# Window attention between two group norms and a 3x3 convolution: v as the weights of the values matmuls, four head pairs side by side

## What is computed

```python
x = x + _L0_conv_ref(_gn(x), qkv_weight, qkv_bias, proj_weight, proj_bias, rel_pos_table)   # attention
x = x + _L1_conv_ref(_gn(x), w, pruning_mask)                                              # 3x3 conv, 128 to 128

# _L0_conv_ref: shifted 7x7 windows; 8 x 8 windows an image, N = 49 tokens each, 8 heads of hd = 16 channels
x = jnp.roll(x, (-3, -3), axis=(1, 2))              # then cut into windows
qkv = x @ qkv_weight.T + qkv_bias                   # q, k, v of each window and head: 49 x 16
q = q * hd ** (-0.5)
attn = jnp.einsum('whnd,whmd->whnm', q, k) + rel_pos_bias + shift_mask
attn = jax.nn.softmax(attn, axis=-1)
x = jnp.einsum('whnm,whmd->whnd', attn, v)          # "values": 49 x 16 for each window and head
x = x @ proj_weight.T + proj_bias                   # windows are put back and rolled back
```

## Time and profile before

| | |
|---|---|
| median of 3 runs | 3634.08 us (3633.68 to 3637.13) |
| profiled execution: its own time | 3628.35 us |
| profiled execution: span, first to last instruction | 3626.5 us |
| granted TensorE clock, mean over the span | 0.995 of full speed |
| busy share PE / DVE / ACT / POOL | 94% / 84% / 73% / 64% |
| instructions in the trace | 141183 |

### The profile page before, as it was taken

One profiled execution on the slowest core, in us unless ns is written; L12 is line 12 of the kernel. 1 busy time (PEld: TensorE's weight loads), 2 busy tenths in 40 slices (PEclk: granted clock), 3 DMA queues, 4 the chain that ended last, 5 costly groups with the idle time before them and its releaser, 6 DMA issues.

```text
span 3626.5 us, 141183 instructions
## 1 busy us (share of the span) xinstructions
PE 3415.0 (94%) x57227; PEld 2799.3 (77%) x57227; DVE 3045.9 (84%) x7552; ACT 2630.5 (73%) x5857; POOL 2322.2 (64%) x3674
## 2 busy tenths in 40 slices
PE   2999999999999999999999999999999999999997
PEld 1778778778778778778777778777778778788785
DVE  5788888888888888888888888888888888888885
ACT  1777777777777777777777777777777777777772
POOL 4476666766666766666766666766667766657763
PEclk9999999999999999999999999999999999999998
DMA  2011101111101111101111111111111111111001
GB/s 57 20 30 33 33 25 30 36 33 36 33 25 30 36 33 36 33 23 33 35 34 35 28 28 33 33 35 36 28 28 33 33 36 33 30 25 33 18 18 29
DMA packets 213331, 113.75 MB, mean 31 GB/s; under 512 B 8784, under 2 KB 212688, under 8 KB 212688
## 3 DMA queue, kind: packets, MB, share of 16 engines
q1 hardware_dynamic: 212688, 104.72, 11.0%
HBM read 53.31 MB, written 51.38 MB: 29 GB/s over the span
## 4 chain that ended last, share of the span: by engine, by line
PE 51%; DVE 23%; POOL 12%; issue 11%; ACT 2%; SPq 0%; DVEq 0%; POOLq 0%; DMA 0%; ACTq 0%
PE conv_ps L994 14%; PE qkv_ps L875 10%; PE attn_ps L913 7%; PE probsT_ps L899 7%; PE scores_ps L888 5%; DVE s_sb L743 4%; POOL s_sb L404 3%; DVE plane_lo L755 3%; PE misc_ps L875 2%; DVE s_max L748 2%; DVE x_b L791 2%; PE misc_ps L961 2%; PE misc_ps L957 2%; PE misc_ps L951 2%; POOL x_n L444 1%
## 5 line engine op out<-in xcount | busy, mean ns | idle before, releaser
L404 POOL TENSOR_TENSOR s_sb<-s_sb,s_max 113x392 f32<-113x392 f32 x1024 | 1027.7, 1004 | 1127.6 <-DVE s_max L748 1123.2
L899 PE MATMUL probsT_ps<-ident,probs 113*128 113x113 f32 x4096 | 586.4, 265 | 72.6 <-ACT probsT L466 72.5
L460 ACT ACTIVATE probs<-s_sb 113x392 f32<-113x392 f32 x1024 | 551.6, 539 | 128.3 <-POOL s_sb L404 124.8
L432 POOL TENSOR_TENSOR plane<-x_n 128x224 f32<-128x224 f32 x896 | 601.3, 692 | 18.7
L913 PEld LDWEIGHTS attn_ps<-v,probsT 128*49 128x49 f32 x16384 | 465.4, 125 | 181.9 <-issue 160.3
L748 DVE TENSOR_REDUCE s_max<-s_sb 113x8 f32<-113x392 f32 x1024 | 574.6, 561 | 35.3
L527 ACT COPY v<-qkv_ps 64x256 f32<-64x256 f32 (+2 forms) x1280 | 393.6, 327 | 287.7 <-PE qkv_ps L875 281.6
L466 ACT COPY probsT<-probsT_ps 128x392 f32<-128x392 f32 x1024 | 489.5, 478 | 144.6 <-PE probsT_ps L899 140.4
L743 DVE TENSOR_TENSOR s_sb<-scores_ps,bias 113x392 f32<-113x392 f32 x1024 | 564.7, 551 | 8.1 <-PE scores_ps L888 8.1
L913 PE MATMUL attn_ps<-v,probsT 128*49 128x34 f32 x16384 | 566.5, 214 | 3.5 <-DVE o_sb L719 0.6
L899 PEld LDWEIGHTS probsT_ps<-ident,probs 113*128 113x128 f32 x4096 | 431.4, 141 | 129.3 <-ACT probs L460 86.0
(11 more groups left out here) (142 smaller groups left out, 6706.9 us busy)
## 6 DMA issues: line engine op xcount, KB each, us to landing
x_in<-in_x_dram SPq DMA_DIRECT2D x224, 224.0 KB, 2.8
out_dram<-x_out SPq DMA_DIRECT2D x224, 224.0 KB, 2.5
x_b<-in_L_conv_w_dram SPq DMA_DIRECT2D x1, 576.0 KB
x_b<-L_conv_pruning_mask_dram SPq DMA_DIRECT2D x1, 576.0 KB
...
```

Of the source, the lines that this page charges most:

```text
L404: nc.gpsimd.tensor_tensor(s, s, top, ALU.subtract).then_inc(sub_ready, 1)
L432: last = nc.gpsimd.tensor_tensor(plane[:, t % 2, j], *sums[j])
L460: nc.scalar.activation(probs[0:QP, slot % 2, :, :, 0:N], s_sb[0:QP, slot % 4], ACT.Exp)\
L899: last = nc.tensor.transpose(probsT_ps[:, w * 128:w * 128 + QP], probs[0:QP, u % 2, w].rearrange("p e m -> p (e m)"), ident[0:QP, 0:QP])
```

## The change

The order of operands in the values product is swapped, and the work is done a row of windows at a time.

- `values(row)` stands once a row of windows, at the end of the row's unit 5 (`VALUES_AT`), for all four head pairs. `v` of one window and pair (32 columns) is the weights, and `probsT` (49 columns) moves. Each pair has its own 32 columns of the array and its own 32 partitions of `attn_ps`, so the output has channels on the partitions at once. 32 matmuls do the outputs. 16 more, with the constant `head_ones` as weights and the `probsT` of two windows (98 columns) moving, add up the softmax's sums for `SUM_PARTS` = 4 pairs of windows in 98 columns of `attn_ps`; `head_ones` puts the sums of part `a` and head `e` on its own partition of the pair's 32 (each four times over).
- DVE takes one reciprocal of 128 x 98 a row (L751). SP writes every fourth partition of it to a DRAM scratch, `recip_dram`, and reads it back into `recip_wide`, spread over the 16 channels of each head and the 392 tokens. DVE multiplies the outputs by it into `o_sb` (L756, unit 8, `NORMED_AT`).
- The `ot` jobs are gone: no transposes. ACT's copy to `oT_hi` stands in the middle of unit 8 and waits for `o_ready`; DVE's `oT_lo` is in unit 9 (`SPLIT_AT`), and `proj` stays at the end of unit 9.
- `probsT` has six slots in place of two, since a row's four units are kept. For the room, `x_out` has two slots in place of seven, and two setup buffers lie inside `plane`. The ones in `v` are gone; POOL writes `head_ones` in the setup.

The core of the diff:

```diff
-LAG_T, LAG_PV = 2, 3
+LAG_T = 2
+VALUES_AT, NORMED_AT, SPLIT_AT = 5, 8, 9
 MID, END = 0, 1
-OT_AT, PROJ_AT = 7, 9
+PROJ_AT = 9
...
+def row_of(i, u, first):
+
+    r, rest = divmod(u - first, PAIRS)
+    turn, r = divmod(r, ROWS)
+    return (i + turn) * ROWS + r if rest == 0 and live(i, turn) else None
...
-        v = sb("v", [128, 2, NWIN, PAIRS, VW])
+        v = sb("v", [128, 2, NWIN, PAIRS, 2 * HD])
         s_sb = sb("s_sb", [128, 4, WP, 2, N])
         s_max = sb("s_max", [128, 4, 2 * WP])
         probs = sb("probs", [128, 2, WP, 2, ODD])
-        probsT = sb("probsT", [128, 2, NWIN, N])
-        recip = sb("recip", [128, 2, 2 * WP, 2])
-        o_sb = sb("o_sb", [128, WP, C])
+        probsT = sb("probsT", [128, PT_SLOTS, NWIN, N])
+        recip = sb("recip", [128, SUM_COLS])
+        recip_wide = sb("recip_wide", [128, RT])
+        o_sb = sb("o_sb", [128, WIN, W])
         oT_hi = sb("oT_hi", [128, WIN, W], F16)
         oT_lo = sb("oT_lo", [128, WIN, W], F16)
+
+        recip_dram = nc.dram_tensor("recip_dram", (2, HEADS, RT), F32).ap()
...
+                    row = row_of(i, u, VALUES_AT + 1)
+                    if row is not None:
+
+                        sp.wait_ge(recip_ready, row + 1)
+                        need(sp, recip_wide_in, 16 * (row - 1))
+                        sp.dma_start(recip_dram[row % 2].rearrange("h (a n) -> (h a) n", a=SUM_PARTS),
+                                     recip[0:128:4, :]).then_inc(recip_out, 16)
+                        need(sp, o_ready, row)
+                        sp.wait_ge(recip_out, 16 * (row + 1))
+                        slot = recip_dram[row % 2]
+                        sp.dma_start(recip_wide[:], bass.AP(tensor=slot.tensor, offset=slot.offset,
+                                                            ap=[[RT, HEADS], [0, HD], [1, RT]]))\
+                            .then_inc(recip_wide_in, 16)
...
+            nc.gpsimd.memset(head_ones[:], 0.0).then_inc(head_consts, 1)
+            pool.wait_ge(head_consts, 1)
+            for e in range(2):
+                for copy in range(PAIRS):
+
+                    diagonal = flat(head_ones)[ODD * e:ODD * e + ODD, e * HD + copy::2 * HD + PAIRS]
+                    nc.gpsimd.memset(diagonal, 1.0).then_inc(head_consts, 1)
+                pool.wait_ge(head_consts, 1 + PAIRS * (e + 1))
...
             def evacuate_probsT(i, g, slot):
                 act.wait_ge(probsT_ready, g + 1)
-                need(act, attn_ready, g - 1)
-                nc.scalar.copy(probsT[:, slot % 2], probsT_ps[:].rearrange("p (w n) -> p w n", n=ODD)[:, :, 0:N])\
+                if g >= PT_SLOTS:
+                    act.wait_ge(attn_ready, (g - PT_SLOTS) // PAIRS + 1)
+                nc.scalar.copy(probsT[:, g % PT_SLOTS], probsT_ps[:].rearrange("p (w n) -> p w n", n=ODD)[:, :, 0:N])\
                     .then_inc(probsT_sb, 1)
...
+                    row = row_of(i, u, NORMED_AT)
+                    if row is not None:
+
+                        act.wait_ge(o_ready, row + 1)
+                        need(act, oT_lo_ready, row)
+                        nc.scalar.copy(flat(oT_hi), flat(o_sb)).then_inc(oT_hi_ready, 1)
...
-                    n, rest = divmod(u - (LAG_PV + 2), 2)
-                    if rest == 0 and live(i, 0 if n >= 0 else -1):
-                        number, half = i * ROWS * 2 + n, n % 2
-                        dve.wait_ge(attn_ready, (number + 1) * 2)
-                        outputs = attn_ps[0:QP, 0:WP * 2 * VW].rearrange("p (a v) -> p a v", v=VW)
-                        vec.reciprocal(recip[0:QP, half], outputs[:, :, 2 * HD:VW]).then_inc(recip_ready, 1)
-                        dve.wait_ge(recip_ready, number + 1)
-                        if half == 0 and (not isinstance(number, int) or number > 0):
-
...
-                        for pair in range(2):
-                            at = (half * 2 + pair) * 2 * HD
-                            last = vec.tensor_tensor(
-                                o_sb[0:QP, :, at:at + 2 * HD].rearrange("p w (e d) -> p w e d", d=HD),
-                                outputs.rearrange("p (w a) v -> p w a v", a=2)[:, :, pair, 0:2 * HD]
-                                .rearrange("p w (e d) -> p w e d", d=HD),
-                                recip[0:QP, half].rearrange("p (w a) e -> p w a e", a=2)[:, :, pair].unsqueeze(3)
-                                .to_broadcast((QP, WP, 2, HD)), ALU.mult)
-                        last.then_inc(attn_norm, 1)
-                    turn, at = divmod(u - 1, UNITS)
-                    for kind, t in misc_at(i + turn, at):
-                        if kind == "ot":
-
-                            row = (i + turn) * ROWS + (t if at >= OT_AT else t - ROWS)
-                            dve.wait_ge(oT_hi_ready, row + 1)
...
+                    row = row_of(i, u, VALUES_AT + 1)
+                    if row is not None:
+
+                        dve.wait_ge(attn_ready, row + 1)
+                        need(dve, recip_out, 16 * row)
+                        vec.reciprocal(recip[:], attn_ps[:, RT:RT + SUM_COLS]).then_inc(recip_ready, 1)
+                    row = row_of(i, u, NORMED_AT)
+                    if row is not None:
+
+                        dve.wait_ge(recip_wide_in, 16 * (row + 1))
+                        vec.tensor_tensor(o_sb[:].rearrange("p r (w c) -> p w r c", c=WIN),
+                                          attn_ps[:, 0:RT].rearrange("p (w r c) -> p w r c", r=WIN, c=WIN),
+                                          recip_wide[:].rearrange("p (w r c) -> p w r c", r=WIN, c=WIN), ALU.mult)\
+                            .then_inc(o_ready, 1)
+                    row = row_of(i, u, SPLIT_AT)
+                    if row is not None:
+
+                        dve.wait_ge(oT_hi_ready, row + 1)
+                        vec.tensor_tensor(flat(oT_lo), flat(o_sb), flat(oT_hi), ALU.subtract).then_inc(oT_lo_ready, 1)
...
-            def values(i, u):
-                g, (r, pair) = i * UNITS + u, divmod(u, PAIRS)
-                pe.wait_ge(probsT_sb, g + 1)
-                if pair == 0:
-                    pe.wait_ge(qkv_free, (i * ROWS + r) * 4 + 4)
-                if pair % 2 == 0:
-                    need(pe, attn_norm, (i * ROWS + r) * 2 + pair // 2)
-                for w in range(NWIN):
-                    p0, wp = ODD * (w % 2), w // 2
-                    at = (wp * 2 + pair % 2) * VW
-                    last = mm(attn_ps[p0:p0 + N, at:at + VW], probsT[:, u % 2, w, :], v[:, r % 2, w, pair, :],
-                              start=True, stop=True)
+            def values(row):
+
+                if row == 0:
+                    pe.wait_ge(head_consts, 1 + 2 * PAIRS)
+                pe.wait_ge(probsT_sb, (row + 1) * PAIRS)
+                pe.wait_ge(qkv_free, (row + 1) * 4)
+                need(pe, o_ready, row)
+                for w, pair in product(range(NWIN), range(PAIRS)):
+                    parts = slice(2 * HD * pair, 2 * HD * (pair + 1))
+                    mm(attn_ps[parts, w * N:(w + 1) * N], v[:, row % 2, w, pair, :],
+                       probsT[:, (row * PAIRS + pair) % PT_SLOTS, w, :], start=True, stop=True)
+                for a, pair in product(range(SUM_PARTS), range(PAIRS)):
+                    parts = slice(2 * HD * pair, 2 * HD * (pair + 1))
+                    last = mm(attn_ps[parts, RT:RT + SUM_COLS], head_ones[:, a, :],
+                              probsT[:, (row * PAIRS + pair) % PT_SLOTS, 2 * a:2 * a + 2, :].rearrange("p w n -> p (w n)"),
+                              start=(a == 0), stop=(a == SUM_PARTS - 1))
                 last.then_inc(attn_ready, 1)
...
-                if kind == "ot":
-                    pe.wait_ge(attn_norm, (i * ROWS + (t + 1 if u >= OT_AT else t + 1 - ROWS)) * 2)
-                    for w in range(WP):
-                        last = nc.tensor.transpose(misc_ps[:, w * 128:w * 128 + QP], o_sb[0:QP, w, :], ident[0:QP, 0:QP])
...
-
+                    pe.wait_ge(oT_lo_ready, i * ROWS + (t + 1 if u >= PROJ_AT else t + 1 - ROWS))
                     hi, lo = (o[:].rearrange("p r w -> p (r w)") for o in (oT_hi, oT_lo))
                     last = three(misc_ps[:, 0:RT], ((wT_hi[:, 3, :], hi), (wT_hi[:, 3, :], lo), (wT_lo[:, 3, :], hi)))
...
-                    late = (u - LAG_PV) % 2 == 0
-                    have_values = live(i, 0 if u >= LAG_PV else -1)
-                    if have_values and not late:
-                        values(i if u >= LAG_PV else i - 1, (u - LAG_PV) % UNITS)
                     if live(i, 0 if u // PAIRS < ROWS - 1 else 1):
                         qkv(i, u)
-                    if have_values and late:
-                        values(i if u >= LAG_PV else i - 1, (u - LAG_PV) % UNITS)
                     conv(i, u, 2)
                     for job in misc_at(i, u, (END,)):
                         misc(i, u, *job)
+                    row = row_of(i, u, VALUES_AT)
+                    if row is not None:
```

(1 more changed line is left out.)

61 lines of the change are left out of this document (28 added, 33 removed).

## The result

The changed kernel takes 3661.32 us (median of 4 runs, 3655.35 to 3668.06) against 3634.77 for the kernel before: ratio 1.0073, 95% interval 1.0054 to 1.0092. It is 0.7% slower. The forecast was 3498. The time lies in the range, on the other side of "no change" from the forecast; the cases that I had put there (a dear values block, a late round trip in every row) are not what happened.

The account below looks back on a forecast made before the run. PE's own stream was taken as the bound, DVE close behind. PE loses 9.4 us an image, half lost to waits: 105.0 against 109.27, 137 us over 32 images, so 3491 profiled and 3498 forecast; range 3420 to 3780.

Parts of the forecast that it names:

- a dear values block: PE's new values block: small matmuls start no faster than now, block 2.55 to 3.03 us, 3740 or 3865; chance 0.22.
- a late round trip in every row: Reciprocal's DRAM trip or ACT's wait for o_ready late in every row, up to 8 us an image; chance 0.1.
- The block: PE's 48 values matmuls a row, four column positions side by side: 1.6 us with the way in.
- The first rival: PE's values block: small matmuls start no faster than now, 26 or 31 ns each, 3740 or 3865 us; chance 0.22.
- The reciprocal: DVE's new reciprocal of 98 columns a row, at 6.3 ns a column: 0.76 us.
- The round trip: recip to DRAM and back as recip_wide: 5.3 us, wide 6.4 us after the block, just hidden by DVE's two units.
- the second rival: Round trip or ACT's wait for o_ready late in every row: 3500 to 3750 us; chance 0.1.
- The pause in the sixth stretch: PE stops about 3.5 us before the block, its copy waiting behind POOL's Newton steps; stretch estimated at 15.6 us.
- `oT_lo` is the nearest row, 0.56 each.: DVE's new multiply and subtraction of 128x392 priced from the old oT_lo row, 0.56 us each.
- The fourth rival: Sixth stretch's 3.5 us pause lowers the granted clock; PE loses some 1.7 us an image, 3554; chance 0.1 of the 0.58.
- For the fifth stretch: Chain of block, reciprocal, DVE, bias and ACT's copy gives 13.1 us, where PE alone would need 12.9.
- Theory F: From the experiments: PE's instructions run out after block and scores until the next 16 KB land; 20 to 30 us.

Follow-up runs that it names:

- e4: Changed kernel with ACT's copy of probsT ahead of the exponential in each unit: 3654.2 us, 1.0060 of the kernel before.
- e12: Changed kernel with only ACT's first tok_hi of the next image one unit later: 3659.6 us, 1.0091 of the kernel before.
- e9: Changed kernel with normalised values left in attn_ps (PSUM) and ACT's probsT copy ahead of the exponential and tok_hi: 3496.1 us, 0.9635 of the kernel before.
- e5: Changed kernel with ACT's probsT copy ahead of the exponential and the next image's first tok_hi one unit later: 3574.9 us, 0.9847 of the kernel before.
- e3: Changed kernel with 16 idle matmuls filling PE's pause ahead of the values block in the sixth stretch: 3643.2 us, 1.0037 of the kernel before.
- e2: Changed kernel without both DMAs of the reciprocals, recip_wide a constant, outputs not normalised: 3645.1 us, 1.0031 of the kernel before.
- e11: The kernel with operand and copy repaired (3496.1 us), values block moved ahead of the projection's three matmuls: 3861.8 us, 1.0645 of the kernel before.
- e6: Changed kernel with the values block in two, the outputs' 32 matmuls moved into the next unit: 3740.3 us, 1.0302 of the kernel before.

## Why the prediction went wrong

**Right.** The block, which held most of my doubt: 1.63 us with the way in, for 1.6. The first rival falls. It had beside it the 60 cycles of overhead for each small matmul (the Trainium skill, TensorEngine Tiling (Array Packing), section Performance Considerations), an estimated 2.4 us for the block; the trace has 1.54. The reciprocal: 764 ns for 0.76. The round trip: from the reciprocal's start to the multiply's it is 6.8 us in the median of the steady part (5.7 to 8.7), for 6.1 and more; leaving it out gave 16 and 19 us, so the second rival falls for the steady part. The pause in the sixth stretch, its place and its 3.2 us. Of its cause the prediction had one half, the exponential behind POOL; the other, `tok_hi`, it did not see, and e4 and e12 show that each of them alone keeps the pause.

**The steps that failed.** By stretch the forecast was 4.1 us an image short (109.1 for 105.0).

"`oT_lo` is the nearest row, 0.56 each." The mis-sized term: 1.01 us. I took the row of the same shape and did not ask where its operands lie. It was worth 2.33 us an image in e9 against e5.

"This ends inside the forecast's range and its chance is part of it (0.1 of the 0.58)." The fourth rival is what happened, and the sum had nothing for it: the clock of the windows is 0.92 and 0.97, and it is low behind the sixth stretch's pause in 28 of the 31 images that have the pause. I had its price right (1.7 us an image; 1.55 measured by e3) and its chance far too low. The 1.1 us pauses that leave the clock at 1.00 were no evidence for one of 3.5 us. Had I put it into the sum, the forecast would have been 3554, as I wrote.

"For the fifth stretch ... 13.1, where PE alone would need 12.9." It is 14.78, and 14.70 in e9, so neither of these two is the cause. I had followed one chain into the block, through the bias and ACT's copy. Another one was longer (timelines of DVE and PE of the changed kernel):

```profile
1794.79 0.15 DVE L716 COPY gn_mean<-misc_ps 128x1 f32<-128x1 f32 x1
...
1794.99 0.34 PE L903 MATMUL misc_ps<-oT_hi,wT_hi 128*128 128x392 f16 x1 [1.03 <-DVE gn_mean L716]
...
1795.59 0.92 PE L940 MATMUL attn_ps<-probsT,v 128*32 128x49 f32 x64
```

The projection waits for `misc_ps`, which DVE frees at the end of its list for this stretch, and the block now stands behind the projection. Before, DVE's release was at 1772.89 and the next scores at 1773.55, 0.7 us later; now it is at 1794.94 and they are at 1797.12, 2.2 us later. The 1.5 us more are about the size of the miss; that they are its cause was read from the trace, not tried.

Not in the forecast at all: the uneven images. Before, the periods of 27 images average 0.05 us over their median; in the changed kernel the mean is 109.85 and the undisturbed image 109.1, some 20 us in all. The first image takes 102.6 us for 88.8. The second rival is part of that: in this image DVE waits for `recip_wide` in seven rows, 13.8 us together, and without the round trip (e2) the image takes 95.5; with ACT's copy free (e5) it takes 97.3. The rest of it was not taken apart.

**The account.** 4.1 x 31 = 127, the uneven images 20, the first image 14: 161 of the 164 us between the 3491 forecast for the profiled execution and its 3655. The first term stands as the sum over the stretches; of it the operand is 2.3 and the clock 1.6 us an image by their experiments, which overlap with the rest in a way that no run separates. With the operand and the copy repaired the kernel takes 3496. That this equals the forecast is partly chance: in e9 the sixth stretch is 3.4 us under its estimate and the fourth, fifth and seventh 3.4 over theirs.

**Open.** Theory F. The eight longest images (110.04 to 112.81 us) all have pauses inside a run of like matmuls, with no semaphore behind them, which the kernel before has none of. The five images of 109.5 to 110.0 have none of over 0.5 us, so the pauses are not all of it (timeline of PE of the changed kernel):

```profile
1095.15 0.55 PE L916 MATMUL scores_ps<-k,q 32*49 32x98 f32 x15
1096.77 0.62 PE L916 MATMUL scores_ps<-k,q 32*49 32x98 f32 x17 [1.08 <-issue]
```

All 20 of over 0.5 us end 2.2 to 2.7 us after the start of a 16 KB load on the instruction queue; that queue makes 514 such loads, one for each 250 of PE's 128790 records. So PE may run out of instructions after block and scores. In the Trainium skill, Runtime: NRT & Kernel Launch, section Instruction fetch mechanics, crossing from one 16 KB block of instructions to the next is mostly hidden; if these pauses are such crossings, 20 of some 514 were not. But e11, with long matmuls between the two, kept 11 of 18 where F said 5 or fewer, and e6 changed more than the density. The cause stays open.
